# A fused attention and ternary feed-forward layer: weights on ScalarE's queue behind the first batch, two passes of quantising, constants in three transfers

## The reference

```python
x = x + xattn(layernorm(x), ctx)      # 8 heads of 16 channels, rotary on the first 8, T = 512
x = x + ffn(layernorm(x))

def act_quant(x):                      # 8 bits, one scale for a token
    scale = 128 / clip(max(abs(x), axis=-1), EPS)
    return clip(round(x * scale), -128, 127) / scale
def weight_quant(w):                   # ternary, one scale for the tensor
    scale = 1.0 / clip(mean(abs(w)), EPS)
    return clip(round(w * scale), -1.0, 1.0) / scale
gate = act_quant(x) @ weight_quant(w_gate).T        # 512 -> 2048
up   = act_quant(x) @ weight_quant(w_up).T
out  = act_quant(fwht(silu(gate) * up)) @ weight_quant(w_down).T
```

## Time and profile before

| | before |
|---|---|
| runs | 1620.98, 1621.62, 1627.97 us; median 1621.62 |
| profiled execution | 1624.36 us, span of its instructions 1622.6 us |
| busy of the span | PE 1481.5 us (91%), DVE 1318.3 (81%), ACT 1125.9 (69%), POOL 848.4 (52%) |
| mean granted TensorE clock | 0.971 |

### The profile page before, as it was taken

The page is one execution under the profiler, slowest core; times in us unless marked ns, Lnnn a source line. Parts: engine busy times, 40 slices in busy tenths (PEclk is TensorE's granted clock), DMA queues, the critical chain, the costliest instruction groups (busy, mean ns, idle before and its releaser), DMA issues.

```text
span 1622.6 us, 26340 instructions
## 1 busy us (share of the span) xinstructions
PE 1481.5 (91%) x8579; PEld 666.8 (41%) x8674; DVE 1318.3 (81%) x2317; ACT 1125.9 (69%) x1841; POOL 848.4 (52%) x648
## 2 busy tenths in 40 slices
PE   1378999999999999999999999999999999999984
PEld 0112344444444444444444434444444444444433
DVE  4477988888888888888888888888888888888741
ACT  4436677777777777777777777777777777777662
POOL 0111665555556655555556655555566555555464
PEclk9568999999999999999999999999999999999997
DMA  5633312233333233223332322323332322333000
GB/s 195 167 111 59 56 44 56 54 57 57 66 66 64 42 59 59 55 56 62 66 66 46 60 56 55 58 56 66 66 64 42 63 53 56 57 50 53 14 7 14
DMA packets 79750, 99.50 MB, mean 61 GB/s; under 512 B 9472, under 2 KB 59904, under 8 KB 78592
## 3 DMA queue, kind: packets, MB, share of 16 engines
q1 hardware_dynamic: 79056, 93.62, 30.1%
q10 hardware_dynamic: 560, 4.19, 0.7%
HBM read 38.80 MB, written 8.39 MB: 29 GB/s over the span
## 4 chain that ended last, share of the span: by engine, by line
PE 75%; DVE 12%; issue 3%; POOL 3%; ACT 2%; DMA 2%; SPq 1%; POOLq 0%; DVEq 0%; ACTq 0%
PE pv L468 15%; PE s L453 14%; PE ring L498 13%; PE s L425 12%; PE ring L543 6%; PE ring L397 6%; PE ring L519 4%; DVE maxima L989 3%; PE ring L477 2%; PE ring L530 2%; DVE h_res L1020 1%; DVE st L1022 1%; DVE attn L1009 1%; DVE turned_pv L999 1%; POOL region L1222 1%
## 5 line engine op out<-in xcount | busy, mean ns | idle before, releaser
L989 DVE TENSOR_REDUCE maxima<-s 128x1 bf16<-128x512 f32 x1024 | 667.0, 683 | 119.9 <-PE s L425 117.8
L688 ACT ACTIVATE region<-s 128x512 f32<-128x512 f32 x1024 | 575.2, 597 | 208.1 <-PE s L453 167.4
L1221 POOL TENSOR_TENSOR region<-region 128x512 f32<-128x512 f32 x192 | 253.3, 1319 | 391.3 <-DVE region L1069 363.8
L425 PE MATMUL s<-region 96*128 96x512 bf16 x1024 | 374.0, 390 | 26.0 <-DMA region<-parts 15.8
L453 PE MATMUL s<-region 97*128 97x512 bf16 x1024 | 352.8, 384 | 5.5 <-ACT region L688 3.0
L468 PE MATMUL pv<-region,v_ext 128*32 128x512 f32 x2048 | 267.2, 605 | 0.5 <-DVE turned_pv L999 0.4
L1222 POOL TENSOR_TENSOR region<-region 128x512 f32<-128x512 f32 x192 | 245.4, 1278 | 0.0
L453 PEld LDWEIGHTS s<-region 97*128 97x128 bf16 x1024 | 95.9, 98 | 240.0 <-ACT region L688 121.2
L425 PEld LDWEIGHTS s<-region 96*128 96x128 bf16 x1024 | 97.6, 97 | 205.8 <-DVE maxima L989 74.7
L1256 POOL TENSOR_TENSOR region<-region,parts 128x1024 f32<-128x1024 f32 x32 | 68.1, 2129 | 175.1 <-ACT parts L755 175.1
L704 ACT ACTIVATE region<-ring 128x512 f32<-128x512 f32 x128 | 76.2, 596 | 116.1 <-PE ring L509 116.1
(11 more groups left out here) (113 smaller groups left out, 1858.1 us busy)
## 6 DMA issues: line engine op xcount, KB each, us to landing
region<-parts SPq DMA_DIRECT2D x768, 64.0 KB
x_in<-in_x SPq DMA_DIRECT2D x32, 256.0 KB, 2.6
c_in<-in_ctx SPq DMA_DIRECT2D x32, 256.0 KB, 2.9
x_res<-in_x SPq DMA_DIRECT2D x32, 256.0 KB, 4.0
out<-o_sb SPq DMA_DIRECT2D x32, 256.0 KB, 4.1
region<-in_wg_t ACTq DMA_DIRECT2D x1, 2048.0 KB, 10.6
region<-in_wu_t SPq DMA_DIRECT2D x1, 2048.0 KB, 7.4
region<-in_wd_t SPq DMA_DIRECT2D x1, 2048.0 KB, 14.8
```

The lines of the kernel that those rows point to most:

```text
L425: pe.matmul(s1[p][:, :], q_stack[k][0:STACK, h, 128 * c:128 * (c + 1)], k_stack[k][0:STACK, h, :], start=True, stop=True).then_inc(s1_full ...
L688: act.activation(probs[:, n % 8, :], s2[n % 2][:, :], ACT.Exp, scale=SCALE).then_inc(exp_done, 1)
L989: dve.reduce_max(maxima[:, c, h:h + 1], s1[p][:, :], AXX).then_inc(s1_max[p], 1)
L1221: pool.tensor_tensor(o[:, :, 0, :], a[:, :, 0, :], a[:, :, 1, :], ALU.add)
```

## The change

The gate, up and down weights are all issued by ACT, behind the constants; up is staged in memory of its own (`probs` and the stack slots of batch 2), so its load waits for nothing, and what uses that memory first waits for up's ternary pieces (`unstaged`, and a wait at the first exponential). Down still takes gate's staging place. Quantising is DVE `round_piece` (times 1/scale, plus ROUND) and ACT `sign_piece` (the sign of what remains after ROUND is taken off). Constants are packed on the host into three arrays. Two rows of ones are set by POOL at the start, the third by DVE. The lists of all engines are written anew, with gate's absolute sums behind batch 0's projections.

```diff
-RING = {"yT1": 3, "down": 3, "zT0": 2, "v": -1, ... "rope": -2, "turn": -2, "pass": -2, "yT0": 2}
+RING = {"yT0": 3, "yT1": 3, "down": 3, "zT0": 2, "v": -1, ... "rope": -2, "turn": -2, "pass": -2}
-FIRST, LAST = -4, B + 4
+FIRST, LAST = -3, B + 5
         def staged(i, j):
             n = 8192 // PIECES[i]
+            if i == 1:
+                if n * j < 4096:
+                    return region[2][:, n * j:n * (j + 1)]
+                return region[n * j // 2048 - 1][:, 6144:8192]
+        def unstaged(engine, b):
+            if b == 2:
+                engine.wait_ge(ternary, UPTO[2])
 # SP
             def load_consts(b):
+                if b == 0:
+                    sp.dma_start(proj_const[:, :], proj_t).then_inc(consts_in, 16)
+                    sp.dma_start(table_const[:, :], table_t).then_inc(consts_in, 16)
             def load_late_consts(b):
+                if b == 0:
+                    sp.dma_start(late_const[:, :], late_t).then_inc(late_consts_in, 16)
-            def load_weights(b, i, h):
-                sp.wait_ge(ternary, UPTO[i - 1] + 2 * (h + 1))
-                load_half(sp, i, h)
             def step(t):
+                stack_part(t, 2)
+                stack_max(t - 1)
+                load_residual(t - 1)
+                load_late_consts(t)
+                load(t + 2)
+                store(t - 4)
+                load_consts(t + 2)
+                stack_part(t + 1, 0)
                 stack_part(t + 1, 1)
 # ACT
+            def load_weights(b, i, h):
+                if b == 0:
+                    act.wait_ge(consts_in, 32)
+                    if i == 2:
+                        act.wait_ge(ternary, 2 * (h + 1))
+                    load_half(act, i, h)
-            def round_piece(b, i, j):
-                act.activation(w, w, ACT.Copy, bias=ROUND, scale=w_inv[:, i:i + 1]).then_inc(w_rounded, 1)
+            def sign_piece(b, i, j):
+                act.wait_ge(w_rounded, UPTO[i] + j + 1)
+                act.activation(piece(i, j, flat(weights[i])), staged(i, j), ACT.Sign, bias=round_neg[:, :])
             def exps(b, n):
+                if n == b == 0:
+                    act.wait_ge(ternary, UPTO[1] + 2)
             def step(t):
...
+                abs_piece(t, 1, 0)
+                sign_piece(t, 0, 1)
+                load_weights(t, 2, 0)
...
                 pass_out(t + 1)
                 first_part(t + 1)
+                abs_piece(t + 1, 0, 0)
+                load_weights(t + 3, 0, 0)
...
+                abs_piece(t, 1, 1)
+                load_weights(t + 1, 1, 1)
+                load_weights(t + 2, 1, 0)
+                sign_piece(t, 0, 2)
+                abs_piece(t, 1, 2)
+                abs_piece(t, 1, 3)
+                second_part(t + 1)
+                sign_piece(t, 0, 3)
+                abs_piece(t, 2, 0)
+                abs_piece(t + 1, 0, 1)
+                load_weights(t, 2, 1)
+                sign_piece(t, 1, 0)
+                abs_piece(t, 2, 1)
+                abs_piece(t + 1, 0, 2)
+                abs_piece(t, 2, 2)
+                sign_piece(t, 1, 1)
+                abs_piece(t + 1, 0, 3)
                 v_out(t + 1)
+                sign_piece(t, 1, 2)
+                load_weights(t + 3, 0, 1)
+                sign_piece(t + 1, 0, 0)
                 max_out(t)
+                abs_piece(t, 2, 3)
                 round_x(t - 1)
+                sign_piece(t, 1, 3)
 # DVE
-            def clip_piece(b, i, j):
-                dve.tensor_scalar(w, w, ROUND - 1, ROUND + 1, ALU.max, ALU.min).then_inc(clipped, 1)
-                dve.tensor_scalar(piece(i, j, flat(weights[i])), w, ROUND, None, ALU.subtract).then_inc(ternary, 1)
+            def round_piece(b, i, j):
+                dve.tensor_scalar(w, w, w_inv[:, i:i + 1], ROUND, ALU.mult, ALU.add).then_inc(w_rounded, 1)
+            def third_ones(b):
+                if b == 0:
+                    unstaged(dve, 2)
+                    dve.memset(k_stack[2][STACK:STACK + 1, :, :], 1.0).then_inc(third_ones_set, 1)
 # POOL
+            pool.memset(round_neg[:, :], -ROUND).then_inc(setup_pool, 1)
+            for k in range(2):
+                pool.memset(k_stack[k][STACK:STACK + 1, :, :], 1.0).then_inc(ones_rows_set, 1)
+                pool.wait_ge(ones_rows_set, k + 1)
             def step(t):
+                hadamard_last(t - 3, 0)
                 mix(t - 2, 0)
-                third_part(t)
                 mix(t - 2, 1)
                 hadamard_last(t - 3, 1)
-                rstd1(t + 1)
                 rstd2(t - 2)
                 hadamard_half(t - 2, 0)
                 rest(t + 1)
                 hadamard_half(t - 2, 1)
-                hadamard_last(t - 2, 0)
+                third_part(t + 1)
+                rstd1(t + 2)
```

More of the change, by code:

```diff
@@ L115, in layer @@
         wd = sb("wd", [128, IC, T], BF16)
[L116 to L123, removed]
+        proj_const = sb("proj_const", [128, 3 * 129], F32)
+        table_const = sb("table_const", [128, 2 * T + 128], F32)
+        late_const = sb("late_const", [128, 4 * 128 + 2], F32)
+        proj_w = {n: proj_const[:, 128 * i:128 * (i + 1)] for i, n in enumerate(("rope", "turn", "pass"))}
+        proj_b = {n: proj_const[:, 384 + i:385 + i] for i, n in enumerate(("rope", "turn", "pass"))}
+        cos_s, sin_s = table_const[:, 0:T], table_const[:, T:2 * T]
+        proj_w["v"] = table_const[:, 2 * T:2 * T + 128]
+        eye, had, wo_c, wo_m = (late_const[:, 128 * i:128 * (i + 1)] for i in range(4))
+        proj_b["v"], proj_b["o"] = late_const[:, 512:513], late_const[:, 513:514]
         eye_b = sb("eye_b", [128, 128], BF16)
@@ L254, in load_half @@
             v = src.rearrange("(c p) n -> p c n", p=128)
[L255 to L261, removed]
+            cut = lambda t, m: t.rearrange("p (c n) -> p c n", c=m)
+            if h == 0:
+                dst = region[2][:, 0:4096] if i == 1 else region[1][:, 0:4096]
+                engine.dma_start(cut(dst, n // 2), v[:, 0:n // 2, :]).then_inc(w_in[i][0], 16)
+                return
+            third, last = (region[1][:, 6144:8192], region[2][:, 6144:8192]) if i == 1 else (region[1][:, 4096:6144], y_last[:, :])
+            engine.dma_start(cut(third, n // 4), v[:, n // 2:3 * n // 4, :]).then_inc(w_in[i][1], 16)
+            engine.dma_start(cut(last, n // 4), v[:, 3 * n // 4:n, :]).then_inc(w_in[i][1], 16)
+        def unstaged(engine, b):
+            if b == 2:
+                engine.wait_ge(ternary, UPTO[2])
         @block.sync
@@ L568, in step @@
                 scores(t - 1, 24)
+                scores(t - 1, 25)
                 score_max(t, 17)
-                scores(t - 1, 25)
                 score_max(t, 18)
@@ L671, in abs_piece @@
                                accum_out=absum[:, UPTO[i] + j:UPTO[i] + j + 1]).then_inc(abs_done, 1)
-            def round_piece(b, i, j):
+            def sign_piece(b, i, j):
                 if b != 0:
                     return
[L676 to L679, removed]
-                act.activation(w, w, ACT.Copy, bias=ROUND, scale=w_inv[:, i:i + 1]).then_inc(w_rounded, 1)
+                if i == j == 0:
+                    act.wait_ge(setup_pool, 3)
+                act.wait_ge(w_rounded, UPTO[i] + j + 1)
+                act.activation(piece(i, j, flat(weights[i])), staged(i, j), ACT.Sign, bias=round_neg[:, :])                    .then_inc(ternary, 1)
             def exps(b, n):
@@ L1307, in _layout @@
         "x": f("x"), "ctx": f("ctx_2048"),
-        "w_rope_t": both(rope), "w_turn_t": both(turn), "w_pass_t": both(rest),
-        "wv_t": wv.T, "wo_t": wo.T, "wo_mix": wo_mix,
-        "b_rope": bias(rope), "b_turn": bias(turn), "b_pass": bias(rest),
-        "bv": col(b_v), "bo": col(b_o),
+        "proj_t": np.concatenate([both(rope), both(turn), both(rest), bias(rope), bias(turn), bias(rest)], axis=1),
+        "table_t": np.concatenate([cos_t, sin_t, wv.T], axis=1),
+        "late_t": np.concatenate([np.eye(128, dtype=np.float32), had, wo.T, wo_mix, col(b_v), col(b_o)], axis=1),
         "wg_t": f("L0_ffn_w_gate").T, "wu_t": f("L0_ffn_w_up").T, "wd_t": f("L0_ffn_w_down").T,
-        "cos_t": cos_t, "sin_t": sin_t, "had_t": had, "eye_t": np.eye(128, dtype=np.float32),
     }
```

321 lines of the change are left out of this document (135 added, 186 removed).

## The result

The changed kernel took 1600.7 us (median of 4 runs, 1598.0 to 1602.5) beside 1621.3 for the kernel before (4 runs) on the same chip: a ratio of 0.986 with a 95% interval of 0.983 to 0.989. The forecast was 1610. The time lies inside the range and the sign was right, but the gain, 20.6 us, is nearly twice the 11.7 of the sum. The profiled execution took 1601.3, its span 1599.5.

The account below looks back on a forecast made before the run. PE was taken to bound the kernel, with the change priced in the first 110 us: 13.2 (to first score product) - 2.5 (to first exponential product) + 1.0 (first steps) = 11.7 us gained, so 1610 us; range 1597 to 1620.

Parts of the forecast that it names:

- the sum: Total gain forecast over the kernel before: 13.2 - 2.5 + 1.0 = 11.7 us, giving 1610 us for the median.
- S: PE's first score product, in the filling stretch; it was at 69.2 us before and forecast near 56.
- the start itself: Ahead of the first score product: POOL's two memsets take 7 to 8 us, first stack copy issued near 19 instead of 43.4.
- Two passes: Quantising in two passes instead of three: DVE loses 14.7 us in all, 1 us of it given back in the first steps.
- the rival of the Sign table: Sign among ACT's exponentials reloads its table, up to 41 us of ACT; kernel slower by 5 to 20 us; chance 0.03.
- Copies go first: Rival: weights do not hold up stack copies, first score product at 40 to 46, total 1597 to 1604; chance 0.17.
- S at 56: Start to first score product: weights and stack copies share the transfer engines, last copy lands near 56 against 69.2; gain 13.2 us.
- S to X: First score product to first exponential product, 37.6 us before: 2.5 us longer (0 to 5), with late maxima behind ACT's pieces.
- X: PE's first product for the exponentials, in the filling stretch; at 106.78 us before, forecast near 96.
- X to batch 2: First exponential product to batch 2's gate product: 1 us gained (0 to 3) of the 4.8 us above steady steps.
- The steady step: PE's repeated step, 45.98 us before: the new order's moves cost nothing; forecast steps of 45.9 to 46.1 us.

## What the prediction had right, and which of its steps failed

**Right.** That PE sets the beat; that much of the change lies in the first 110 us (12.4 of the 23.1 between the spans); that weights in another queue take the engines from the copies, so that starting them 24 us earlier brings S forward by much less; the rate of the weights, 375 GB/s for 374; the start itself (memsets, first copy at 19); the constants worth nothing by themselves in the total, though not at S. Two passes cost what the nearest rows said: rounding took 1.28 us, as the clip pass that it was priced by (1.23), and sign 1.99 for 1.9. ACT's groups of the kernel after:

```profile
L681 ACT ACTIVATE wu<-region,round_neg 128x2048 bf16<-128x2048 f32 x4 | 8.0, 1990 | 3.1 <-DVE region L943 3.1
...
L750 ACT ACT_TABLE_LOAD x1 | 1.3, 1283 | 16.0 <-PE ring L392 16.0
```

One table load, so the rival of the Sign table falls. "Copies go first" falls too, as 61 packets beside weights show; 1600.7 lies in its range of times because other terms moved.

**S at 56: down's first half was not ahead of the copies.** The step that failed is "11.0 MB at 375 GB/s (between the 357 here and 403 at its best) is 29.3 us, and 19 of stack copies". Of the 11.0 MB, 2.10 are down's first half, 5.6 us. They were added as if they went ahead of the copies, though by the prediction itself ACT reaches that load near 39.5 and gate and up end near 33. They landed 5 us behind S, and the run in which they wait has S at 50.1. Without them the same sum is 7.5 + 8.91 MB at 375 GB/s (23.8) + 19 = 50.3 us, and S came at 50.7 and 48.2. That it fits to half a microsecond is luck: the drain of the copies is no constant, and seven profiles with these loads have S from 45.1 to 55.6 (see the last section).

**S to X: the wrong wait.** The prediction had 2.5 us from ACT's pieces ahead of the maxima, and they came 87.69 - 50.68 = 37.0 us behind S where it was 35.6 before: 1.4 later, less than that. But it followed the maxima only. Moving down's second load to ACT's queue put it among batch 1's copies, which PE needs ahead of X, and PE stood 7.48 us. The prediction prices weights beside the copies of batch 0 only; down's second half and batch 1's copies are in none of its terms. The runs with that load elsewhere show it: the wait is gone in all three, and with the 2 MB behind the maxima S to X is 38.1.

**X to batch 2: 1 for 4.5 us.** The three steps were 4.8 us longer than steady ones; now they exceed them by 0.8. "Of which I give 1 back" was too careful. The third pass put back returns 2.2 of it in one profile, though profiles without it differ by up to 1.7 in this stretch; three shorter steps are 0.5. For the other 1.8 no run has a cause.

**The steady step: 0 for 4.4 us.** This is the second step that failed, "I cost them at nothing". It was costed by asking what the moves could delay, and not what they could save. 0.16 us a step is 4.4 over 27. Parting the projection block again costs 0.26 us, so the joining of these products is a cause large enough; that it is the cause was not shown, and the exchange of PE's whole list could not say it.

**The cancelling.** In the spans, 5.3 us more at S, 3.5 in the first steps, 4.4 in the steady ones and the tail's 1.8 stand against 3.6 for the missed wait: 11.4 more than the sum, and less the 2.5 by which the executions stand to their medians some 9 more than forecast. The version that takes the missed wait away and also holds up's weights back is 8.6 us faster; by the two profiles 5.2 of that lie between S and X and 3.7 at S.

## What to carry to other kernels

When a bulk load is moved to another queue, count it ahead of a small transfer only if it is issued before that transfer is through. List every small transfer of every batch that will be in flight with it, not only those of the batch in mind, and place it behind the one whose consumer is next on the bound engine. Price a new order in both directions: a tenth of a microsecond in a step is 3 us in 29.

## What the runs showed of the hardware

- Bulk weights hold back 1 KB copies without stopping them: 61 packets in 3 us beside 137 of weights, 323 without. An 8 KB transfer issued 0.6 us behind a load of 2 MB on another queue took 5.4 us instead of 1.94.
- Copies from SBUF to SBUF drained at different rates from one execution to the next. In seven profiles with the same loads ahead of S, 261 to 430 packets passed from 33 to 36 us (323 and 394 in the two of the changed kernel). The engines' share was 0.56 to 0.58 in all of these, so a packet took longer, 63 to 107 ns (share x 16 engines x 3 us by packets). S lay between 45.1 and 55.6 us in them. No run shows the cause, and a difference of a few microseconds at S between two profiles proves nothing.
